# Perceiver layer on one core: VectorE's fifth context place in a refill step, placed behind the eviction of the turned queries

## The reference, cut to what matters

```python
ln = layernorm(layernorm(x)) * ln_w + ln_b
qx = layernorm(fp8_linear(ln, wqx))              # 8 groups x 2 heads x 128 wide
kx, vx = split(einsum('bsi,oi->bso', ctx, w_kv_x))
kx = layernorm(kx)                               # per group, 128 wide
xout = softmax(qx @ kx.T * 128 ** -0.5) @ vx     # 1601 context rows
core = the same attention of ln over its own batch's 64 tokens
x = x + fp8_linear(concat([core, xout]), wproj)
```

## Time and profile before

| what | value |
|---|---|
| median of three runs | 2190.99 us |
| the profiled execution: its own time | 2188.6 us |
| its span | 2187.3 us |
| DVE, ACT, POOL busy | 53%, 43%, 30% of the span |
| TensorE's granted clock, mean | 0.952 of full speed |
| DMA | 255.73 MB, mean 117 GB/s |
| attention steps | from about 155 to 1797 us of the span |

### The profile page before, as it was taken

How to read it: one execution, slowest core, us unless ns; L and a number is a source line. 1 busy time by engine, 2 the same in 40 slices (tenths; PEclk the granted TensorE clock), 3 DMA queues, 4 the chain that set the end, 5 groups by cost and what they waited for, 6 DMA issues and landing times. The chain is left out here.

```text
span 2187.3 us, 30639 instructions
## 1 busy us (share of the span) xinstructions
PE 1976.7 (90%) x10424; PEld 1667.4 (76%) x10424; DVE 1154.9 (53%) x2672; ACT 938.6 (43%) x1787; POOL 654.7 (30%) x707
## 2 busy tenths in 40 slices
PE   3899999999999999999999999999999984758758
PEld 3678888888888888888888888888888873631536
DVE  6564454445444554455344545454554435968854
ACT  4554354444433443444344434443443434617321
POOL 3224543222233223222222322233223213510331
PEclk9999999999999999999999999999999996879769
DMA  6675344434332433344333434343432226400020
GB/s 193 198 235 162 116 141 124 153 92 143 114 119 82 141 118 116 103 142 132 103 116 116 134 89 129 111 149 91 141 118 82 77 67 216 191 21 3 1 77 20
DMA packets 213130, 255.73 MB, mean 117 GB/s; under 512 B 62120, under 2 KB 132392, under 8 KB 212464
## 3 DMA queue, kind: packets, MB, share of 16 engines
q1 hardware_dynamic: 202480, 252.92, 37.1%
q10 hardware_dynamic: 8448, 0.43, 0.2%
q0 software_dynamic: 2048, 0.43, 0.1%
HBM read 222.32 MB, written 30.83 MB: 116 GB/s over the span
## 5 line engine op out<-in xcount | busy, mean ns | idle before, releaser
L478 PE MATMUL kx_ps<-ctxT_hi,wk_hi 128*128 128x400 f32 (+1 forms) x1024 | 375.6, 367 | 10.0 <-DVE ctxT_lo L288 8.7
L482 PE MATMUL kx_ps<-ctxT_hi,wk_lo 128*128 128x400 f32 (+1 forms) x1024 | 361.3, 353 | 0.0
L480 PE MATMUL kx_ps<-ctxT_lo,wk_hi 128*128 128x400 f32 (+1 forms) x1024 | 360.3, 352 | 0.0
L564 PE MATMUL u_ps<-ctxN_hi,pt_hi 128*128 128x512 f32 (+1 forms) x832 | 341.9, 411 | 3.3 <-DVE pt_lo L760 3.3
L565 PE MATMUL u_ps<-ctxN_lo,pt_hi 128*128 128x512 f32 (+1 forms) x832 | 330.4, 397 | 0.0
L566 PE MATMUL u_ps<-ctxN_hi,pt_lo 128*128 128x512 f32 (+1 forms) x832 | 329.2, 396 | 0.0
L698 DVE TENSOR_TENSOR kx_lo<-kx_ps,kx_hi 128x400 fp32r<-128x400 f32 (+1 forms) x256 | 146.8, 574 | 307.4 <-ACT sq L938 307.4
L760 DVE TENSOR_TENSOR pt_lo<-t_ps,pt_hi 128x512 fp32r<-128x512 f32 (+1 forms) x256 | 145.2, 587 | 294.4 <-ACT pt_hi L971 294.2
L936 ACT ACTIVATE kx_hi<-kx_ps 128x400 fp32r<-128x400 f32 (+1 forms) x256 | 129.2, 505 | 394.7 <-PE kx_ps L482 391.7
L971 ACT ACTIVATE pt_hi<-t_ps 128x512 fp32r<-128x512 f32 (+1 forms) x256 | 126.7, 529 | 324.4 <-PE t_ps L548 324.2
L478 PEld LDWEIGHTS kx_ps<-ctxT_hi,wk_hi 128*128 128x128 f32 x1024 | 198.7, 194 | 13.2 <-DVE ctxT_lo L288 9.0
(11 more groups left out here) (248 smaller groups left out, 3640.8 us busy)
## 6 DMA issues: line engine op xcount, KB each, us to landing
rstd_bc<-scratch_rstd SPq DMA_DIRECT2D x64, 804.0 KB, 5.7
stage<-in_ctx_t SPq DMA_DIRECT2D x96, 267.0 KB, 4.7
stage<-in_ctx_n SPq DMA_DIRECT2D x96, 256.0 KB, 6.1
wk_hi<-scratch_wk_s SPq DMA_DIRECT2D x56, 256.0 KB, 2.8
wk_lo<-scratch_wk_s SPq DMA_DIRECT2D x56, 256.0 KB, 3.1
wv_hi<-scratch_wv_s SPq DMA_DIRECT2D x56, 256.0 KB, 4.0
wv_lo<-scratch_wv_s SPq DMA_DIRECT2D x56, 256.0 KB, 4.7
scratch_own_rows<-out_sb SPq DMA_DIRECT2D x32, 256.0 KB, 3.0
```

Source lines behind the costliest of these rows:

```text
L478: PE.matmul(kx_ps[:, j % 2, 0:w], wk_hi[:, g % 2, i, :], ctxT_hi[:, i, c0:c0 + w], start=(i == 0), stop=False)
L480: PE.matmul(kx_ps[:, j % 2, 0:w], wk_hi[:, g % 2, i, :], ctxT_lo[:, i, c0:c0 + w], start=False, stop=False)
L482: mm = PE.matmul(kx_ps[:, j % 2, 0:w], wk_lo[:, g % 2, i, :], ctxT_hi[:, i, c0:c0 + w], start=False, stop=(i == C - 1))
L564: PE.matmul(u_ps[:], pt_hi[0:w, t % 2, cols], ctxN_hi[0:w, y, :], start=(y == 0), stop=False)
```

## The change

VectorE's place 4 moves: its two subtractions no longer stand between `keys_low(n+3, 0)` and the output's eviction, but behind `query_out(n+2)`, ahead of `keys_low(n+3, 1)`. Nothing is added or removed. The order of ScalarE, TensorE, GpSimd and SyncE is unchanged.

```diff
@@ -893,7 +893,6 @@
                 refill(3)
                 if k:
                     keys_low(n + 3, 0)
-                refill(4)
                 if v:
                     b, g = divmod(n, G_)
                     V.wait_ge(o_done, n + 1)
@@ -907,6 +906,7 @@
                         own_less_maximum(u)
                     if r:
                         query_out(n + 2)
+                refill(4)
                 if k:
                     keys_low(n + 3, 1)
                 if 3 <= n + 4 < G_:
```

## The result

The changed kernel takes 2155.11 us (median of 4 runs, 2153.37 to 2158.54) against 2192.14 us before (4 runs); the ratio is 0.9835, 95% interval 0.9818 to 0.9852. It is faster by about 37 us. The prediction said 2153.

What follows compares the result with a forecast made beforehand. TensorE, busy 90%, was held at L523 by the late query eviction and ensuing clock falls. 9.9 + 13.4 - 0.5 + 15.3 - 1.6 = 36.5 us off 2188.6 gives 2152.1, or 2154.5 against the median; forecast 2153, range 2146 to 2171.

Steps and rivals of the forecast that it cites:

- The eviction: VectorE's eviction of the turned queries ends at 327.69, before TensorE reaches L523 at 328.59; the wait goes whole.
- The new wait of g = 5: At L478, keys(n+3, 2) waits 0.9 us for piece 11; 1.41 of 2.31 us remain, 9.9 us over seven steps.
- The cover of g = 7: Piece 23 stays hidden at L564 by 0.26 us; batches 2 to 7 gain 13.4 us, less 0.5 for small misses.
- one sign that the prediction named for being wrong: L564 waiting in the later batches; the prediction expected its long idle only in the first batch.
- The first batch's g = 7: At L564, no gain: the wait for piece 23 lengthens from 1.40 to 5.2 us, with one clock fall, -1.6 us.
- The clock: TensorE's clock falls behind L523 go: six in g = 5 at 1.5 us, four in g = 7 at 1.57, 15.3 us.
- a rival of chance 0.10 that they stay: The clock's falls behind L523 stay, so the time is 2153 + 15.3 = 2168 us; chance 0.10.
- The sum: Whole kernel: 9.9 + 13.4 - 0.5 + 15.3 - 1.6 = 36.5 us gained against the profiled execution's 2188.6.
- the term for g = 7: In steps g = 7 of batches 2 to 7, L523's wait goes: 6 x 2.24 = 13.4 us, less 0.5.

Runs made afterwards that it cites:

- e5: Kernel before, with ScalarE making the high parts of place 4 ahead of the exponentials, VectorE's order unchanged; 2155.20 us, ratio 0.9836.
- e6: Changed kernel, with SyncE in steps g = 7 issuing the loads of pieces 23 and 24 ahead of the weights; 2147.23 us, ratio 0.9801.
- e2: Kernel before, with the two subtractions moved in the seven steps g = 7 only; 2167.96 us, ratio 0.9903.

## Why the prediction was right

*The eviction.* Forecast: L523 without idle in all 14 steps, since VectorE has time for the eviction while it waits for ScalarE. So it was, and e5 shows the cause from the other side.

*The new wait of g = 5.* Forecast 0.9 us from the last L478 of one group of keys to the first of the next, beyond the undisturbed 0.68. Measured 330.11 - 328.53 = 1.58, a loss of 0.90. The profile's own idle is 0.75; the remaining 0.15 us is what TensorE loses beyond the idle when it starts again, as before, where 2.31 us were lost for an idle of 2.04. The step from L523 to L523 was given as 25.6 and is 25.76 (329.08 to 354.84): there I had added an idle time and a difference of starts, which differ by this loss at the start.

*The cover of g = 7* held in four of the six batches and missed in two. The steps behind g = 7 take 25.1 us in batches 2, 3, 6 and 7, and 25.32 and 25.86 in the fourth and fifth, where L564 waits 0.23 and 0.42 us and, in the fifth, L495 0.31 us. In the fourth batch, for which the sum had 0.26 us to spare, the issue of piece 23 stayed where it was, as forecast, but its transfer took 6.33 us (992.70 to 999.03) instead of 5.79 (1008.64 to 1014.43), and the chain behind it 2.26 us instead of 2.10. So one sign that the prediction named for being wrong, L564 waiting in the later batches, did appear. It cost about 1 us in all; the term was 0.5, its bounds 0 and 6.

*The first batch's g = 7.* Forecast: no gain, an idle of 5.2 us, one fall of the clock. Measured 4.69 us and one fall, at 398 us. With the 0.65 us of the later start taken off, TensorE came to L564 0.3 us later than summed, and the chain behind piece 23 ended 0.3 us earlier. From L523 of n = 6 to that of n = 8 it takes 56.79 us instead of 55.53: 1.3 us lost, the term was 1.6. e6 shows that the wait was SyncE's, handed on through a transfer.

*The clock.* Forecast: the falls go, 15.3 us, with a rival of chance 0.10 that they stay. They went. The table of the Trainium skill named in the prediction ("TensorE: Matmul & The Clock Gate", table "Why this matters for your kernels") names only longer idle gaps as a cause, and taken as the only cause it would have them stay. But 19 of 28 waits of 2.0 us had a fall behind them and none of 14 at 1.2 us, so here the measurement decides against that reading. What the prediction did not know is that 2.0 us lies in the middle of the range, so that the number of falls before was not fixed by the waits: with three falls fewer in g = 5, as in e2, this term would have been 5 us smaller. That it came out so close is in part luck.

*The sum* was 36.5 us. The attention steps of the profiled executions give 36.5, the medians 37.0. That the first agrees to the tenth is luck: the term for g = 7 was half a us too large, the first batch lost 0.3 us less than summed, the six falls in g = 5 were worth 1.49 to 1.62 us each and not 1.5 (about 0.3 us in all), and the part behind the steps varies by more than all of these. That 2153 is only 2 us off is in part luck too: the time before was 2190.99 in the median of the first three runs and 2192.14 in that of four.

## What to carry to other kernels

An in-order engine that waits for a slow neighbour holds up every finished piece of work behind the wait. Look for engines that stand idle ahead of work for which all inputs are there, and ask who waits for that work; VectorE was busy only half the time here, and its order still set TensorE's pace. On a kernel like this, count an idle of TensorE of 1.5 us or more twice, once as time and once as a chance of a fall of the clock, and follow each removed wait to the next, here one instruction further on.

## What the runs showed of the hardware

I had not expected the clock's falls to depend so gradually on the idle: 0 of 14 at 1.2 us, 1 of 14 at 1.5, 19 of 28 at 2.0, 14 of 14 at 3.4. One fall costs 1.5 to 1.6 us here and a double one about 1.2 us more. As an estimate from these counts, a wait of 2.0 us costs 3.1 us on average, idle and clock together, and one of 3.5 us about 5.5. How the chip decides in a single case is open: equal waits in equal steps of one kernel had both outcomes, and no run here separates the two. The counts come from one execution of each kernel, so the shares between none and all are rough.
